# Block-diagonal keys of 16-wide heads: eight scaled evictions replaced by one eviction and eight SBUF-to-SBUF transfers on ScalarE's queue

## The reference

```python
q = split_heads(queries @ Wq + bq)
k = split_heads(keys @ Wk + bk)
v = split_heads(values @ Wv + bv)
scores = jnp.einsum('bhqd,bhkd->bhqk', q, k) / jnp.sqrt(jnp.float32(HD))
scores = jnp.where(mask, jnp.float32(-1000000000000000.0), scores)
attn = jax.nn.softmax(scores, axis=-1)
ctx = jnp.einsum('bhqk,bhkd->bhqd', attn, v)
return ctx @ Wo + bo
```

## Time and profile before

| | |
|---|---|
| runs, us | 2932.72, 2942.46, 2941.31 |
| median, us | 2941.31 |
| profiled execution, first to last instruction (the only time known of it), us | 2934.9 |
| PE busy / PEld | 2558.6 us (87%) / 1872.8 us (64%) |
| DVE busy | 1775.3 us (60%) |
| ACT busy | 1337.9 us (46%) |
| POOL busy | 809.9 us (28%) |
| l0x, first to last score matmul, us from the start | 257.1 to 415.1 |
| l1a | 589.0 to 743.9 |
| l2fa | 1790.2 to 1933.9 |
| l3x | 2337.2 to 2501.5 |

### The profile page before, as it was taken

The page is one execution under the profiler, slowest core; times in us unless marked ns, Lnnn a source line. Parts: engine busy times, 40 slices in busy tenths (PEclk is TensorE's granted clock), DMA queues, the critical chain, the costliest instruction groups (busy, mean ns, idle before and its releaser), DMA issues. The chain is left out here.

```text
span 2934.9 us, 48117 instructions
## 1 busy us (share of the span) xinstructions
PE 2558.6 (87%) x16117; PEld 1872.8 (64%) x16117; DVE 1775.3 (60%) x4091; ACT 1337.9 (46%) x3461; POOL 809.9 (28%) x627
## 2 busy tenths in 40 slices
PE   5998989999688779699998998977969888869997
PEld 2666756767455446467776776757955566449896
DVE  7876886588788634444444657873346588434443
ACT  2333654256777323434333445743432388324442
POOL 5533530054100134122211224641110044142222
PEclk8999999999877789799999999988989999889999
DMA  9001000000200423200001002042130300531110
GB/s 322 4 0 50 14 19 1 14 3 1 65 5 1 87 67 110 90 1 1 1 1 40 22 1 73 2 147 85 37 91 1 85 15 5 174 123 52 51 52 27
DMA packets 152052, 142.44 MB, mean 49 GB/s; under 512 B 59948, under 2 KB 136770, under 8 KB 151428
## 3 DMA queue, kind: packets, MB, share of 16 engines
q1 hardware_dynamic: 139668, 110.61, 12.9%
q0 software_dynamic: 10560, 27.19, 2.7%
q10 hardware_dynamic: 1584, 1.57, 0.2%
HBM read 98.14 MB, written 43.02 MB: 48 GB/s over the span
## 5 line engine op out<-in xcount | busy, mean ns | idle before, releaser
L962 POOL TENSOR_TENSOR room<-room 128x1024 f32<-128x1024 f32 x144 | 274.0, 1903 | 432.2 <-DVE room L895 431.9
L1435 PE MATMUL l3f_out<-room,Y 128*128 x624 | 141.1, 379 | 0.0
L889 DVE TENSOR_REDUCE room<-room 128x8 f32<-128x1024 f32 (+1 forms) x144 | 139.9, 971 | 0.7 <-ACT room L1038 0.7
L962 POOL TENSOR_TENSOR room<-room,Y 128x1024 f32<-128x1024 f32 x32 | 60.7, 1898 | 252.0 <-DVE Y L895 252.0
L1435 PEld LDWEIGHTS l3f_out<-room,Y 128*128 128x128 f32 x624 | 115.6, 190 | 14.1
L1036 ACT ACTIVATE room<-l2a_scores,Y 128x128 f32<-128x128 f32 x256 | 72.1, 381 | 86.6 <-DVE Y L881 86.6
L2478 POOL DMA_INDIRECT sorted_rows<-room,l1f_place_i x32 | 31.0, 968 | 279.7 <-DVE l1f_place_i L2189 270.8
L607 PE MATMUL l2a_proj<-room 128*128 128x256 f32 x384 | 97.5, 398 | 11.6 <-ACT room L986 11.6
L1036 ACT ACTIVATE room<-l1a_scores,room 128x128 f32<-128x128 f32 x256 | 71.6, 386 | 58.4 <-DVE room L881 58.4
L1036 ACT ACTIVATE room<-l0x_scores,room 128x128 f32<-128x128 f32 x256 | 70.7, 385 | 59.2 <-DVE room L881 59.2
L607 PEld LDWEIGHTS l2a_proj<-room 128*128 128x128 f32 x384 | 71.8, 196 | 24.7 <-issue 14.9
(11 more groups left out here) (842 smaller groups left out, 7084.3 us busy)
## 6 DMA issues: line engine op xcount, KB each, us to landing
sorted_rows<-head SPq DMA_DIRECT2D x1, 16640.0 KB, 57.2
room<-in_L_ffn_w SPq DMA_DIRECT2D x16, 1024.0 KB
room<-in_L_ffn_W SPq DMA_DIRECT2D x16, 1024.0 KB
Y<-sorted_rows SPq DMA_DIRECT2D x62, 130.0 KB
room<-in_ctx SPq DMA_DIRECT2D x24, 256.0 KB, 2.7
room<-sorted_rows SPq DMA_DIRECT2D x39, 130.0 KB
room<-results SPq DMA_DIRECT2D x8, 512.0 KB, 7.1
room<-in_L_ffn_routed_w SPq DMA_DIRECT2D x4, 512.0 KB
```

Of the source, the lines that this page charges most:

```text
L889: dve.tensor_reduce(rsum[:, u % 2, 0:SUMMED], p[:, u % (TURN + 1), 0:SUMMED, :], AX.X, ALU.add)
L962: pool.tensor_tensor(p[:, u % (TURN + 1), :, :], p[:, u % (TURN + 1), :, :], rinv[:, u % (TURN + 1), :].unsqueeze(2).to_broadcast([P, HEAD ...
L1435: mm = pe.matmul(obank[n % 2][:, 0:D], hT[:, n % 2, f, :], chip.room[:, bass.ds(at + (SLOT // 2 + f * D), D)], start=(f == 0), stop=(f == ...
```

## The change

For `small` plans the keys are evicted once, by ACT, into a new buffer `kT` of [P, C, PT] (one buffer, not two): two instructions with the bias, one copy without. Then ACT's queue issues eight transfers, one for each o and each half of 64 partitions: 16 partitions, two chunks, two batches, 128 floats each (32 KB), from `kT` to their place in `kB`. The zeros of `kB` are written once per block, by a DVE memset of 4096 columns ahead of `consts_ready`. The table `bkB` goes. PE's score of a pair's first step now waits for the semaphore `k_spread` of the eight transfers instead of the eviction.

```diff
             if small:
-                return kind == "q" or (kind == "k" and plan.mask == "timebias")
+                return kind in "qk"
...
                     if t % PER == 0:
-                        for f in ks + qs:
+                        for f in qs if small else ks + qs:
                             wait_emptied(pe, (g, f))
+                        if small:
+                            pe.wait_ge(k_spread[g % 2], (g // 2 + 1) * 16 * 2 * UNIT)
...
-                if "bk" in w.v and small:
-                    for c in range(C):
-                        op = dve.tensor_scalar(bkB[:, c, :], own[:, 0:UNIT], w.v["bk"][:, c:c + 1], None, ALU.mult)
+                if small:
+                    dve.memset(kB[:, :, :, :, :], 0.0).then_inc(kB_zeroed, 1)
...
-                    if kind == "k" and small:
-                        for c in range(i, i + per_bank):
-                            for o in range(UNIT):
-                                op = dve.tensor_scalar(kB[:, g % 2, c, :, o * P:(o + 1) * P], ...
...
+                def spread(x):
+
+                    g, (kind, i) = x
+                    if kind != "k" or not small:
+                        return
+                    wait_emptied(act, x)
+                    if g == 0:
+                        act.wait_ge(kB_zeroed, 1)
+                    for o in range(UNIT):
+                        for a in range(2):
+                            rows = slice(64 * a + 16 * o, 64 * a + 16 * o + 16)
+                            act.dma_start(kB[rows, g % 2, :, :, o * P:(o + 1) * P], kT[rows, :, :].rearrange("p c (j t) -> p c j t", j=PAIR)).then_inc(k_spread[g % 2], 16)
+
                 for f in opening:
                     if by_scalar(f):
                         empty((0, f))
+                        spread((0, f))
...
                     if t < T:
                         exps(t, 1)
+                    for x in at[(t, 0)]:
+                        spread(x)
...
                         act.copy(oT[:, b % 2, st * CS:(st + 1) * CS, :], ...
+                    for x in at[(t, 1)]:
+                        spread(x)
```

More of the change, by code:

```diff
@@ L464, in attention_block @@
             kB = sb("kB", [P, 2, C, PAIR, UNIT * P])
+            kT = sb("kT", [P, C, PT])
             v = sb("v", [P, VB, PAIR, VSLOTS * 32])
@@ L507, in attention_block @@
         v_zeroed = sem("v_zeroed")
+        kB_zeroed = sem("kB_zeroed")
+        k_spread = [sem("k0_spread"), sem("k1_spread")]
         stats_ready = sem("stats_ready")
@@ L784, in empty @@
                     m = number[x]
-                    if kind == "k" and small:
-                        for c in range(i, i + per_bank):
-                            for o in range(UNIT):
-                                op = dve.tensor_scalar(kB[:, g % 2, c, :, o * P:(o + 1) * P], bank[:, (c - i) * PT:(c - i + 1) * PT].rearrange("p (j t) -> p j t", j=PAIR),
-                                                       w.v["bk"][:, c:c + 1] if "bk" in w.v else 0.0, own[:, o:o + 1], ALU.add, ALU.mult)
-                    elif kind == "k":
+                    if kind == "k":
                         if "bk" in w.v:
@@ L988, in empty @@
                         op = act.copy(cT[:, :, :], whole)
[L989 to L997, removed]
                     elif kind == "k":
+                        dst = kT if small else kT[:, g % 2, :, :]
                         if "bk" in w.v:
                             for c in range(i, i + per_bank):
-                                op = act.activation(kT[:, g % 2, c, :], whole[:, c - i, :], ACT.Identity, bias=w.v["bk"][:, c:c + 1])
+                                op = act.activation(dst[:, c, :], whole[:, c - i, :], ACT.Identity, bias=w.v["bk"][:, c:c + 1])
                         else:
-                            op = act.copy(kT[:, g % 2, i:i + per_bank, :], whole)
+                            op = act.copy(dst[:, i:i + per_bank, :], whole)
                     elif kind == "q":
@@ L1044, in _ @@
                         exps(t, 0)
+                    for x in at.get((t - 1, 2), []):
+                        spread(x)
                     for x in at[(t, 0)]:
@@ L1049, in _ @@
                         exps(t, 1)
+                    for x in at[(t, 0)]:
+                        spread(x)
+                    if t < T:
                         if plan.mask == "support":
```

2 lines of the change are left out of this document (removed).

## The result

The changed kernel takes 3036.15 us (median of 4 runs, 3027.93 to 3038.63) against 2937.01 us of the kernel before in the same comparison: a ratio of 1.0326, 95% interval 1.0307 to 1.0345. The profiled execution has a span of 3035.9 us, 101.0 more than that of before. It is slower, as forecast, and by twice as much: the forecast was 49 us more, with an upper end of 3025.

A forecast was written before the change was run, and what follows sets the result against it. PE was taken to bound l0x, l1a and l2fa, with no engine full in l3x. Steady losses of 33.7 us and openings of 15.6 made 49 us, added to 2941.3 for 2990 us, range 2955 to 3025.

The forecast's parts named there:

- the issue: ACT's queue, each pair: .51 us a transfer, 4.1 us for eight (3.0 to 5.4), with nothing behind them on ACT starting meanwhile.
- the relief of the evictions: DVE in l0x, l1a and l2fa: evictions of 29.4 us a block go, worth nothing in the steady part.
- The openings: Starts of the four blocks: memset, issue and landing delay first scores by 6.6, 5.0, 3 and 1, sum 15.6 us.
- What bounds the kernel: l0x, l1a and l2fa run at PE's pace, with 12 us of PE idle; in l3x no engine is full.
- rival A: All four blocks: issuing nearly free on ACT, 8 and 10 idle us regained, openings keep 5; 2928 us, chance 7%.
- rival D: ACT's queue: .67 us an issue because short four-dimensional pieces go slower, ACT full in l2fa; 3031 us, chance 15%.
- Rival A's point of decision: ACT in l1a: at about 0.2 us an issue the hole equals its 3.76 us of idle time less the eviction.
- That nothing runs beside the issues: ACT: no computation goes on while its queue issues; the prediction is wrong if ACT goes on computing.
- The steady losses by block: Seven pairs each in l0x, l1a, l2fa and l3x: 1.5, 7.7, 13.3 and 11.2 us, sum 33.7.
- the two waits of PE: l3x, each pair: score 0.95 us later, projection of v 2.2 later; 1.6 taken, as PE wins some back.
- rival E's mechanism: Openings or first scores of each pair wait for transfers landing late behind prefetched weights; 3002 us, chance 5%.
- the two cases for the sequencer's time: ACT's queue: either issuing is small relative to the transfer, steady cost nothing, or eight issues outlast one landing.

The follow-up runs named there:

- Experiment 4: Buffer laid out so each transfer writes 16 pieces of 2 KB instead of 64 of 512 bytes, against the changed kernel: 3027.92 us.
- experiments 3 and 10: Only four, respectively six, of the eight transfers a pair kept, against the changed kernel: 2941.44 us and 2980.36 us.
- experiment 5: DVE's memset of the buffer moved behind the signal that lets ACT begin, against the changed kernel: 3040.58 us.
- experiment 1: The same eight transfers a pair issued from SP's queue instead of ACT's, against the changed kernel: 2945.08 us.

## Why the prediction was right in its sign and wrong in its size

**The steps that failed.** Three terms of the sum were wrong: the issue was mis-sized (.51 us, measured .64), the lower clock that follows PE's gaps in l3x had no term, and the relief of the evictions was put at nothing (measured 20.8 us, the other way). The openings were short by 5.5.

**What bounds the kernel: half right.** PE is the bound in l0x, l1a and l2fa, and a hole in ACT's queue that reaches it is not won back. But "worth nothing in the steady part" failed for the evictions. Without transfers the steady part is 20.8 us shorter than before. It was read off one pair in which PE did not notice; the 12 us of idle time that the forecast itself counted were there to be spent, and rival A, which did spend some, put 18 us there. Of the 14.5 us gained in the three blocks 7.8 were idle time; the rest was PE's busy time, which the forecast took as fixed.

**The issue time: the term that was mis-sized.** Taken at .51 us each, 4.1 for eight; measured .64, 5.12 to 5.14, in some pairs up to 6.47 (l0x) and 6.60 (l3x's opening). The bounds held it (.38 to .67), the choice was wrong: the row of eight equal transfers of 32 KB in a run was the nearest one, and I moved away from it because its pieces were shorter. Experiment 4 shows that the pieces do not matter between 16 and 64. With 5.13 in the forecast's own working each of the four losses rises by 1.03 us, 7 times, which is 29 us, and the openings by 4: 82 us instead of 49. That sum is near the 89.5 measured, but by luck: it would put 14.9 and 20.5 us in l1a and l2fa and 8.7 in l0x, as the blocks below show. The far end was cut off for the same reason: rival D, at 3031, had nearly the right number with 15%, and its reason (short pieces in four dimensions) was the wrong one. Its remark that ACT would be full in l2fa came nearer: 103.8 us busy and seven holes of 3.8 to 4.4 us make 131 of 145. Rival A's point of decision, 0.2 us an issue, does not follow from its own numbers: 3.76 less 0.9, divided by eight, is 0.36. The slack of some 2 us a hole in experiments 3 and 10 puts it at about a quarter of a microsecond (an estimate).

**That nothing runs beside the issues: nearly right.** It was one of the forecast's signs of being wrong, and it is there in part: one to two issues are covered by exponentials already handed over, in l1a above, where 4.16 us of 5.12 are left, and in l2fa, where 3.8 are. In l0x nothing is left to cover.

**The steady losses by block.** Forecast 1.5, 7.7, 13.3 and 11.2 for l0x, l1a, l2fa and l3x; measured 15.0, 10.6, 14.5 and 28.3. In l1a and l2fa the mechanism and the size of one pair were right, since a longer issue and the cover offset each other: PE's turn waits 1.24 and 2.0 us where 1.1 and 1.9 were forecast. That the sums of these blocks came out near as well is partly luck, since the unforeseen relief, 3.1 and 5.9 us, was set off by other waits and by PE's longer busy time (2.9 and 7.0 us above that of the run without transfers). In l0x the step was .2 us a pair, with the score just in time; with 5.12 of issue the same working gives 1.2, and the scores wait 1.36 us behind each such run but the first pair's (4.50, 2.58 before); behind runs of 5.57 (the row above), 5.73 and 6.47 they wait 1.81, 1.98 and 2.72. So l0x failed by the issue time, the first pair and 2.9 us of longer busy time. In l3x the two waits of PE were named, but added to 1.6 of 4.0 measured (2.80 and 1.23 above, against .41 before). And no term stood for the clock: in the l3x windows a PE instruction takes 126 ns on the average instead of 115, which for 1135 of them is 13 us, next to 12 us more idle time. PE's gaps are what the lower clock follows: it is .85 with eight transfers, .91 with six, .95 with four or in portions, .97 with none.

**The openings.** Forecast 15.6, measured 21.1 (l0x 5.8, l1a 3.6, l2fa 6.2, l3x 5.4 against 6.6, 5.0, 3 and 1). In l0x and l1a it was the memset that was overrated: 3.47 us instead of 4.0, and mostly beside PE's first projections (in l1a it held the first eviction by 1.6, experiment 5). ACT starts its first eviction in l0x at 248.59, against 249.01 in the earlier trace rows; counted from the last matmul of the sublayer before, which ended 1.7 us earlier, that is 1.3 later and not 3.4. In l2fa it was the landing, rival E's mechanism in one place. In l3x it was the issue: eight took 6.60 us, and ACT's root for the statistics (line 252) stands behind them, on which DVE and then PE's projection of the time bias wait. By the forecast's own working, 6.6 less the 2.4 that the evictions free, that alone is 4.2. The timelines of l1a, l2fa and l3x:

```profile
601.71 3.47 DVE L755 MEMSET room<- 128x4096 f32 x1
...
605.31 0.84 ACT L989 ACTIVATE room<-l1a_proj,vecs 128x256 f32<-128x256 f32 x2 [13.03 <-DVEq L758]
606.18 5.14 ACTq L1014 DMA_DIRECT2D room<-room  x8
...
612.87 1.01 PE L657 MATMUL l1a_scores<-causal_b,ident_b 128*128 128x512 bf16 x2 [4.67 <-DMA room<-room]
...
1830.31 5.23 ACTq L1014 DMA_DIRECT2D room<-room  x8
...
1841.42 2.08 PE L663 MATMUL l2fa_scores<-room 64*128 64x256 f32 x8 [9.10 <-DMA room<-room]
...
2398.80 6.60 ACTq L1014 DMA_DIRECT2D room<-room  x8
2405.45 0.22 ACT L252 ACTIVATE std<-var 128x16 f32<-128x16 f32 x1 [6.67 <-issue]
...
2407.25 3.78 PE L625 MATMUL l3x_proj<-upper,room 128*128 128x128 f32 x16 [5.03 <-DVE room L823]
```

In l1a the scores start 1.5 us after the last issue, in l2fa 5.9, while the weights of the next block are on their way. The usual landing is shorter than the 2.4 us taken from the earlier trace rows; the DMA issues by line (size, median us to landing):

```profile
room<-room ACTq DMA_DIRECT2D x256, 32.0 KB, 2.0
```

**What was right.** The place and the order: eight issues on ACT, the copy late in l1a and l2fa, the scores late in l0x, the projection of v late in l3x, DVE 72.4 us less busy in all (24 a block, 26 forecast), the landing hidden in the steady part. Of the two cases for the sequencer's time the trace bears out the row: one issue, .64 us, is about a third of the 2.0 us to the landing of its transfer, and eight, 5.1, are longer than one landing. The rule of the Trainium skill that the forecast weighed ("DMA: Bandwidth & Descriptors", section "Issuing engines are not separate DMA queues"), that this time is usually small relative to the transfer, is not borne out here as a price of nothing. Moving the issues from ACT to SP, where no computation stands behind them, is worth 91 us (3036.15 to 2945.08). The Trainium skill, in "Perfetto Trace Analysis", section "DMA Optimizations", says that balancing transfers over the engines that can issue them may help if generating descriptors is the bottleneck; experiment 1 is in line with that, though here all 256 went to one other queue, and what the issues held up was ACT's computation.

## What to carry to other kernels

Price a transfer first by what its issue takes on the engine that issues it, times their number, and look at what stands behind it on that engine; use an engine with nothing behind it, or cut the run into portions that are no longer than the slack of one step. Where rows differ, take the one with the same number and size of transfers, and doubt a reason for moving away from it. Small transfers that somebody waits for must not follow large prefetches.

## What the runs showed of the hardware that was not expected

- A transfer of 32 KB within SBUF costs .63 to .64 us of issue on ACT and on SP alike, and on ACT with 16 pieces of 2 KB as with 64 of 512 bytes (5.00 and 5.12 us for eight).
- ACT goes on with up to four exponentials that it already holds while its queue issues: 2.53 us of issues left a hole of 1.45.
- Behind four weights of 1 MB the issue itself slows down: eight transfers took 9.27 us on SP instead of 5.05 to 5.13, and the first of them 4.49.
- In l3x gaps of 2.80 and 1.23 us in PE went with 6.8 us at a granted clock of .50, in which a projection took 1.97 instead of 1.10 us.
